# Reordering the first tiles of the second pass: transposes, projections and a bias add in a two-layer graph kernel

## What is computed

```
deg = maximum((adj != 0).sum(-1), 1)
# layer 0
pooled = dinv * (adj + eye) * dinv @ x + x          # dinv = rsqrt(deg)
x = layernorm(x + relu(pooled @ W + b))
# layer 1
type_sum = adj @ x
attn_a, attn_b = sigmoid(concat([type_sum, x]) @ Wa.T + ba), the same with Wb, bb
h = x @ W_sa ; scores = (h @ a_left)[:, None] + (h @ a_right)[None, :]
e = where(adj != 0, exp(-leaky_relu(scores, 0.01)), 0)
x_a = e / (e.sum(1) + 1e-5) @ h ; x_b = adj @ (x @ W_gcnb) + b_gcnb
x = layernorm(x + sigmoid(attn_a * x_a + attn_b * x_b))
```

## Time and profile before

| | us |
|---|---|
| median of 3 runs | 879.18 |
| lowest, highest | 878.85, 879.31 |
| the profiled execution, span from first to last instruction | 877.3 |
| TensorE, busy matmuls | 856.7 |
| VectorE busy | 683.4 |
| ScalarE busy | 571.2 |
| GpSimd busy | 181.3 |

### The profile page before, as it was taken

The page is one execution under the profiler, slowest core; times in us unless marked ns, Lnnn a source line. Parts: engine busy times, 40 slices in busy tenths (PEclk is TensorE's granted clock), DMA queues, the critical chain, the costliest instruction groups (busy, mean ns, idle before and its releaser), DMA issues.

```text
span 877.3 us, 20460 instructions
## 1 busy us (share of the span) xinstructions
PE 856.7 (98%) x7579; PEld 755.0 (86%) x7579; DVE 683.4 (78%) x1182; ACT 571.2 (65%) x1214; POOL 181.3 (21%) x181
## 2 busy tenths in 40 slices
PE   8899999999999998999999999999999999999997
PEld 7787888888888887887788888888888888888886
DVE  5787676766667567898988988988978978978863
ACT  5754555555555237988977976966966967867831
POOL 1001333323322321012022022032032032032021
PEclk9999999999999999999999999999999999999999
DMA  9989999998999424110220120120120220220001
GB/s 321 305 273 320 352 401 339 360 344 315 380 316 341 174 105 144 56 55 1 79 80 15 63 78 24 54 78 15 63 78 6 71 78 0 78 78 0 25 25 37
DMA packets 66617, 130.01 MB, mean 148 GB/s; under 512 B 5464, under 2 KB 29056, under 8 KB 62080
## 3 DMA queue, kind: packets, MB, share of 16 engines
q1 hardware_dynamic: 57632, 120.87, 39.2%
q10 hardware_dynamic: 8928, 8.38, 2.8%
HBM read 99.87 MB, written 29.36 MB: 147 GB/s over the span
## 4 chain that ended last, share of the span: by engine, by line
PE 76%; issue 11%; DVE 5%; ACT 3%; DMA 3%; POOL 1%; SPq 0%; POOLq 0%; ACTq 0%; DVEq 0%
PE ps L1529 31%; PE ps L1365 21%; PE ps L1470 19%; PE ps L1400 4%; ACT ec L624 2%; DVE ec L1099 1%; DMA xs<-in_x_dram 1%; ACT em L633 1%; DMA h_scratch<-hst 1%; PE ps L1385 1%; DVE em L1106 1%; DVE dd L940 0%; POOL zb L434 0%; DMA x1r<-x_scratch 0%; SPq L335 0%
## 5 line engine op out<-in xcount | busy, mean ns | idle before, releaser
L1529 PE MATMUL ps<-fb,em 128*128 128x257 f16 x3072 | 347.5, 273 | 0.8 <-DVE em L1106 0.8
L1529 PEld LDWEIGHTS ps<-fb,em 128*128 128x128 f16 x3072 | 300.5, 98 | 38.6 <-issue 1.3
L1365 PE MATMUL ps<-y,codes 128*128 128x257 f16 x2048 | 237.8, 273 | 0.4 <-DVE y L831 0.4
L1365 PEld LDWEIGHTS ps<-y,codes 128*128 128x128 fp8e4 x2048 | 200.2, 98 | 27.0 <-DVE y L831 0.8
L624 ACT ACTIVATE ec<-slb,nsb 128x256 f32<-128x256 f32 x512 | 211.3, 499 | 0.0
L1106 DVE SCALAR_TENSOR_TENSOR em<-ec,em 128x2048 f16<-128x2048 f32 x64 | 147.4, 2303 | 22.7 <-ACT em L633 22.7
L633 ACT ACTIVATE em<-ec 128x2048 f16<-128x2048 f32 x64 | 122.1, 1910 | 65.1 <-PE ps L1529 57.0
L1099 DVE SCALAR_TENSOR_TENSOR ec<-ec,pan 128x2048 f32<-128x2048 f32 x64 | 147.3, 2302 | 2.6 <-issue 1.8
L1470 PE MATMUL ps<-zz,dd 128*128 128x256 f16 x768 | 89.4, 273 | 1.5 <-DVE t L1128 1.3
L458 POOL TENSOR_TENSOR sc<-sc,sc 128x2 f32<-128x2 f32 x15 | 38.5, 2569 | 246.3 <-DVE sc L1208 246.3
L1470 PEld LDWEIGHTS ps<-zz,dd 128*128 128x128 fp8e4 x768 | 75.0, 98 | 10.7 <-issue 2.0
(11 more groups left out here) (154 smaller groups left out, 786.0 us busy)
## 6 DMA issues: line engine op xcount, KB each, us to landing
strip<-in_adj_dram SPq DMA_DIRECT2D x128, 512.0 KB, 7.5
a_scratch<-codes SPq DMA_DIRECT2D x16, 1024.0 KB, 10.3
pan<-a_scratch SPq DMA_DIRECT2D x16, 1024.0 KB, 4.9
x_scratch<-x ACTq DMA_DIRECT2D x32, 128.0 KB, 5.3
x1r<-x_scratch SPq DMA_DIRECT2D x16, 256.0 KB, 2.8
h_scratch<-hst ACTq DMA_DIRECT2D x30, 136.0 KB, 5.5
out_dram<-ot SPq DMA_DIRECT2D x15, 256.0 KB, 2.2
fb<-h_scratch SPq DMA_DIRECT2D x3, 1088.0 KB, 8.8
```

The source lines that it names most:

```text
L1365: mm = pe.matmul(ACC(n), codes[:, qq % SLOTS, h, jb, e * P:(e + 1) * P].bitcast(F8), y[:, jb, part, 0:YC], start=(jb == 0 and part == 0), ...
L1529: mm = pe.matmul(PH(2 * m + e)[:, 0:HC], em[:, c, e_part, i, e * P:(e + 1) * P], fb[:, jb, h_part, 0:HC], start=(jb == 0 and e_part + h_pa ...
```

## The change

Three places are reordered; no instruction is added or removed.

- GpSimd: z_with_bias(n + 2) is issued ahead of the wait for the statistics of tile n and of its power, for all tiles.
- ScalarE and VectorE, tiles 0 to 3: ScalarE copies the transposed tile n + 1 ahead of proj_copies(n). VectorE takes x1t_lo(n - 1) between residual(n) and stats(n), and h_lo(n - 2) between stats(n) and normalize(n).
- TensorE, tiles 4 and 5: p_step(j) and t_step(j + 1) stand together behind quarters 1 and 3, instead of one behind each quarter.

```diff
             for n in range(T):
                 ln = lnst[:, n % 2, :]
+                if n + 2 < T:
+                    z_with_bias(n + 2)
                 pool.wait_ge(S["stat_ready"], n + 1)
                 pool.tensor_tensor(ln[:, RS], ln[:, VE], sc[:, MH], ALU.pow).then_inc(S["rstd_ready"], 1)
-                if n + 2 < T:
-                    z_with_bias(n + 2)
...
             cast(3)
             x1t_copy(0)
             cast(1)
+            x1t_copy(1)
             proj_copies(0)
-            x1t_copy(1)
             cast(1)
+            x1t_copy(2)
             proj_copies(1)
-            x1t_copy(2)
             forms_hi(0)
             cast(1)
+            x1t_copy(3)
             proj_copies(2)
-            x1t_copy(3)
             proj_copies(3)
             cast(3)
...
+            def first_head(n):
+                degree(n)
+                residual(n)
+                x1t_lo(n - 1)
+                stats(n)
+                if n >= 2:
+                    h_lo(n - 2)
+                normalize(n)
+
             head(0)
             normalize(0)
-            head(1)
-            x1t_lo(0)
-            normalize(1)
+            first_head(1)
             cast(1)
-            head(2)
-            h_lo(0)
-            normalize(2)
-            x1t_lo(1)
+            first_head(2)
             cast(2)
-            head(3)
-            h_lo(1)
-            x1t_lo(2)
-            normalize(3)
+            first_head(3)
             forms_lo(0)
             cast(1)
+            x1t_lo(3)
             h_lo(2)
-            x1t_lo(3)
             cast(1)
...
                 if n == PT:
-                    between = {0: ((p_step, 0),), 1: ((t_step, 1),), 2: ((p_step, 1),), 3: ((t_step, 2),)}
+                    between = {1: ((p_step, 0), (t_step, 1)), 3: ((p_step, 1), (t_step, 2))}
                 elif n == PT + 1:
-                    between = {0: ((p_step, 2),), 1: ((t_step, 3),), 2: ((p_step, 3),)}
+                    between = {1: ((p_step, 2), (t_step, 3)), 3: ((p_step, 3),)}
```

## The result

| | before | after |
|---|---|---|
| median, us | 879.24 (878.85 to 880.9, 4 runs) | 885.96 (885.17 to 886.22, 4 runs) |
| ratio | | 1.006, 95% interval 1.0044 to 1.0077 |
| profiled execution, span | 877.3 | 884.1 |

The change is slower by 0.6% (the ratio is the recorded one, with its interval; the two medians alone give 1.0076, at the upper end of it). The forecast was no measurable change, 879.5 us, with a range of 878.0 to 881.0: the time lies outside.

The account below looks back on a forecast made before the run. TensorE, busy 98%, bounds the kernel; only its early waits count, ceiling some 3.6 us. Tile 4's transposes +0.5 us, less 0.2 at its projection, net +0.3: 879.18 + 0.3 = 879.5 us, range 878.0 to 881.0.

Parts of the forecast that it names:

- T0 0.3 earlier: TensorE's transposes of tile 0 start at 75.5 us, a gain of 0.3, through a normalization shortened by 0.4.
- Nothing behind GpSimd's moved wait matters: On GpSimd, no queue behind the moved wait was to matter, since the power follows later anyway.
- Waits of p0 and p1 gone, a new one of 1.4 for strip 29: TensorE's projections of tiles 0 and 1 stop waiting for L946; adjacency matmuls wait 1.4 us for VectorE's codes.
- T2 11.55 behind T0: TensorE's transposes of tile 2 start at 87.05 us instead of 87.8, with those of tile 0 at 75.5.
- h(0) issued 12.4 behind T0: ScalarE sends h(0) to DRAM at 87.9 us instead of 83.33, behind the copy of tile 2 and x1's DMA.
- h(0) takes 8.6 us: h(0)'s DMA lands at 96.5 us, 8.6 after issue, with bounds of 3.5 and 10.6; projection of tile 3 waits 1.9.
- rival 2: h(0) takes as long as the codes, 10.6 us, landing 98.5; tile 4's transposes +2.5 us, time 881.7; chance 0.12.
- From landing to p3 1.25: From h(0)'s landing through L576 and L933 to TensorE's projection of tile 3: 1.25 us, starting at 97.75.
- From p3 to T4 3.9 us: From tile 3's projection to tile 4's transposes the chain takes 3.9 us, TensorE's work 3.1; transposes start at 101.7.
- p4's old wait of 0.2 gone: TensorE's projection of tile 4 finds x1t_lo(4) ready, where it lost 0.2 us before.
- No wait after 106 us but T4's: No TensorE waits appear after 106 us; all later work moves with the shift of tile 4's transposes, corrected at its projection.
- rival 1: h(0) lands within 7 us, by 94.9; tile 4's transposes shift -0.9 to -1.4, time 878.2; chance 0.26.

Follow-up runs that it names:

- pool_only: Kernel before with only GpSimd's edit, the bias added ahead of the power; median 880.4 us, ratio 0.9994.
- three_after: Changed kernel with three buffers hst instead of two; median 881.0 us, ratio 1.0006 to the kernel before.
- three_casts: Changed kernel with three buffers hst and VectorE's casts of strips 29 and 31 moved up to that of 27; median 880.9 us, ratio 0.9985.
- h0_late: Kernel before with only h(0)'s DMA put behind ScalarE's copy of transposed tile 2; median 888.1 us, ratio 1.0082.
- after_again: Changed kernel unaltered, timed again on another chip beside the kernel before; median 885.3 us, ratio 1.0049.
- h0_first: Changed kernel with two adjacent ScalarE DMAs swapped, h(0) sent ahead of x1(2); median 882.6 us, ratio 1.0013 to the kernel before.
- pool_three: Kernel before with GpSimd's edit and three buffers hst, no other reordering; median 880.4 us, ratio 0.9992.
- wts_before: Kernel before with the small weights loaded behind strip 2 instead of strip 4; median 881.2 us, ratio 1.0005.

## Why the prediction was wrong

Times in the kernel after are relative to T0 at 78.16, forecast ones to T0 at 75.5.

- **T0 0.3 earlier:** right (14.09 against 14.37 behind S). L990 is 0.41 where it was 0.81.
- **Nothing behind GpSimd's moved wait matters:** wrong, though it did not decide. GpSimd's sums L278 to L280 stand behind it, and pool_only gained 1.4 us of rest where the prediction gave this edit 0.3. In the kernel after, p3's wait for h(0) covered the part over the sums.
- **Waits of p0 and p1 gone, a new one of 1.4 for strip 29:** right, 1.32.
- **T2 11.55 behind T0:** 11.63. **h(0) issued 12.4 behind T0:** 12.43, right.
- **h(0) takes 8.6 us: wrong, 10.9.** This is the step that failed, a term of the sum: the latency of h(0), which sets p3's wait. The prediction read the rows of transfers after codes (7.1 to 9.1) and took a value among them. But a latency counted from issue depends on when it was issued: in the kernel before x1(2), sent at 88.22, landed 8.5 us later at 96.7, and h(1), sent 3.15 later, at 99.2, so 2.5 behind x1(2); its 7.8 is short only since it was sent late. h(0) was now to stand right behind x1(2). h(0)'s packets need another 2.8, by the prediction's own count; sent 0.4 later, that makes 8.5 + 2.8 - 0.4 = 10.9 us. The same rows held the right number, and the text had both halves of it; that they meet to a tenth is partly luck. Where the traces have both landings, x1(2) took 8.1 to 9.0 us and h(0) landed 1.8 to 2.8 behind it (1.8 in three_after, 2.3 in three_casts, 2.8 in h0_late). What the rows didn't show in one piece is the 4.5 us without any packet. The term was +2.3 us of the miss, and it is rival 2's condition (10.6).
- **From landing to p3 1.25:** right, 102.81 - 101.56 = 1.25.
- **From p3 to T4 3.9 us: wrong, 5.57.** TensorE's clock fell after the 4.06 us of standing still, and p3 took 2.75 for 1.49, +1.25. The prediction gave a wait of TensorE its length as price and no more: this is the second term that was mis-sized. The other 0.3 to 0.4 are the normalization of tile 4: it was taken at 0.42, and took 0.76, since after p3's delay it met GpSimd's sums L280:

```profile
107.57 0.76 DVE L990 TENSOR_SCALAR x<-x,lnst 128x256 f32<-128x256 f32 x1
```

```profile
107.54 0.63 POOL L280 TENSOR_TENSOR fs<-gb 128x256 f32<-128x256 f32 x1
```

- **p4's old wait of 0.2 gone:** right (T4 to p4 3.80 for 3.99).
- **No wait after 106 us but T4's:** right; whatever T4 loses, the span loses.

Together: -0.3 at T0, then forecast +0.8 from T0 to T4, +0.1 at T2, +2.3 latency, +1.65 from p3 to T4, -0.2 at p4, and that is +4.35 for the +4.1 of the rest. The forecast mechanism and its place were right; rival 2 described what happened, with a price of 2.5 that lacked the clock. It got a chance of 0.12 because the packet counts of a stretch in which the queue already moved were read as the rate of the whole latency. The range was too narrow for the same reason: its upper end of 881.0 left out the bound of 10.6 us that the text itself gave (881.7), and a fallen clock would have put that at 883.

The remaining 2.4 to 2.7 us of the first pair, 6.7 in all, are not the change's: in the two profiles they arose before the first changed instruction, and against 29 runs of the kernel before it was 4.3 us (after_again). They are the start's scatter, which 3 runs of the kernel before (878.85 to 879.31) did not show.

**The Trainium skill's rule** in "DMA: Bandwidth & Descriptors", section "Queues, rings and completion order", that an engine drains a packet of some 9 to 17 descriptors from one queue before it switches, was rightly not followed for the time: rival 1, which it would have given, did not come. With work in both queues the counts were 104 and 102, and in h0_first, with 128 packets fewer ahead of it, h(0) came 2.3 us sooner. Whether the 4.5 us without a packet are such a turn of SyncE's queue, no run here shows.

The Trainium skill, "SBUF — State Buffer", section "Who interferes with whom", says that an operation of VectorE or GpSimd that takes the ports they share keeps the other out for its whole length; the trace agrees for L990 that the two hinder one another, 0.76 to 0.83 us beside an addition or product on GpSimd and 0.40 to 0.42 without. It doesn't show the whole length: at 74.92 in the kernel before the addition overlaps L990 by 0.66 us, and L990 is 0.4 longer.

## What to carry over

A transfer's latency is a property of its place: when it is put behind another in the same queue, add its own packets to the predecessor's landing, rather than take a mean of measured latencies. Before moving a wait or a copy ahead of a step, list the DMAs which that step begins with and who needs their buffers back: here swapping two of them gave back 3.6 of 4.1 us, and a third buffer all of it. And price a wait of TensorE with the slower clock that may follow it, here another 1.3 to 2.9 us in the runs in which it fell.

## What the runs showed of the hardware

- **A queue without a packet.** ScalarE's two transfers, issued 1.2 and 1.6 us behind the second of two 1 MB writes' issue, had no packet until 4.5 us after the first was issued, while SyncE's queue had 233 in 2 us. With both moving it was one for one (104 and 102). The same transfer took 2.3 us when issued before those writes, 8.6 behind them, and 10.0 to 10.9 behind them and an x1. What the queue waits for in those 4.5 us is open.
- **TensorE's clock after a wait.** Behind waits of 2.33 and of 3.4 to 5.87 us near tile 5, rows ran at or near the lower level (1.2 GHz) for 3 to 6 us; in h0_late p3's 12 and the next 32 matmuls lost 2.9 us. Behind waits of 1.10 to 1.72 us there they were at full speed. At the start the length of one wait does not decide it. The clock fell behind one of 2.00 us in h0_late (1.91 us for a row that takes 1.03), and it stayed up behind one of 2.99 in pool_three and one of 2.57 in wts_before. TensorE in h0_late, then in pool_three:

```profile
29.06 0.22 PE L1426 MATMUL ps<-ident,wrow 8*128 8x8 f32 x1 [2.00 <-DMA sc<-in_L_gnn_bb_dram]
...
30.52 1.91 PE L1353 MATMUL ps<-w,xt 128*128 128x256 f32 x4
```

```profile
29.81 0.22 PE L1422 MATMUL ps<-ident,wrow 8*128 8x8 f32 x1 [2.99 <-DMA sc<-in_L_gnn_bb_dram]
...
31.08 1.03 PE L1349 MATMUL ps<-w,xt 128*128 128x256 f32 x4
```

  Windows of h0_late (columns as above):

```profile
103.00:106.00 3.00, 3.00 (x15) 2.09 (x14) 2.67 (x9) 0.37 (x2) 0.00 (x0) 0.50 0.16 58
106.00:109.00 3.00, 3.00 (x18) 2.15 (x16) 1.87 (x5) 2.97 (x8) 2.93 (x5) 0.56 0.00 0
```
